# Identity products in half of the array's rows, the bias table in two passes of transfers, and two normalisations on GpSimd

## The chip, the cores and the metric

The kernel runs on one core of a Trainium2 chip. The metric is the device time of one launch in microseconds. Of the kernel before there are three runs, 289.52, 291.94 and 294.78 us (median 291.94), and one profiled execution of 286.88 us, whose span (first to last instruction) is 285.0 us.

## The reference

One transformer block in float32 on x of 8 batches x 256 tokens x 128 features:

```
n = layernorm(x)
q, k, v = split(n @ W_qkv + b_qkv)                  # 16 heads of 8
scores = q @ k.T / sqrt(8) + bias[head, i - j]      # rel_bias, clipped at +-128
y = softmax(scores) @ v @ W_out + b_out
x = x + layernorm(y)
h = silu(x' W1 s1) * (x' W2 s2)                     # x' = layernorm(x), ternary weights, 512 wide
h = gelu(h H1 s); h = gelu(h H2 s)                  # 512 x 512
x = x + layernorm(h W3 s)
```

## The kernel before, in words

**Stages.** A prologue (to about 34 us) normalises x, makes q and k in the layout that the scores need, and takes the row maxima of the scores of batch 0. Then seven loop passes b = 0 to 6 of eight slots s = 0 to 7 (a slot is a pair of heads) compute the attention of batch b and, beside it, the row maxima for batch b + 1. A last stage (about 173 to 190 us) does the attention of batch 7, and the feed-forward part (from about 190 us) works in four chunks of 512 tokens.

**One slot.** TensorE does, in this order: the scores of (b, s) on top of the bias (`scores`, L1325); the plain scores of (b + 1, s) (`max_scores`, L1291); the bias on top of these by a product of an identity with the table (`max_bias`, L1299); and then something that differs from slot to slot: the weighted sums of a group of four heads (`weighted`, L1351), transposes (`back`, `heads_T`, `norm_T`, `maxima_T`), the output projection (`project`, L1375), or in b = 0, 2, 3, 4 pieces of the q, k and v of later batches. L1325 and L1291 contract over 33 rows, at rows 0 and 64 of the array for the two heads of a pair; the identity product contracts over all 128 rows, two products of 512 columns in a slot.

VectorE takes the row maxima of the finished tile (`maxima`, L703). Then the tile is free for the bias of a later slot, copied from the table `raw` in SBUF by ScalarE (`write_bias`, L1053) or, in the slots of `BY_DVE`, by VectorE (L710). ScalarE takes the exponential of the scores (`probabilities`, L1046). There are three PSUM tiles `place`: ScalarE's copy of slot s waits for the maxima of slot s - 2, and the plain scores of slot s wait for the exponential of slot s - 1.

**Beside it.** In each pass b > 0 VectorE also finishes batch b - 1: `weigh` in s = 1, 2, `attn_moments` in s = 4 (adds the output bias, mean and variance), `residual` in s = 5 (normalises y, adds it to x, and takes mean and variance of the sum), `second_norm` in s = 6. GpSimd computes the inverse deviations between them (`inv_std`, L525), and in the pauses splits the feed-forward weights into a high and a low part (`split_weights`, eleven pieces, four instructions each, in the passes that `SPLIT_AT` gives).

**The table.** `ext` holds for each head one row of the bias by distance; `raw` is 128 partitions x 16 heads x 384, partition p shifted by p, loaded in eight transfers of 384 KB (L392) at the start. `table_hi` is its rounded copy in the format that the identity product reads, made by GpSimd (`table_high`, L533).

All engines run their lists in the order in which they are written, and so does SyncE, which issues nearly all transfers. Each PSUM tile, buffer and result has a semaphore.

## Time and profile before

| | us |
|---|---|
| runs | 289.52, 291.94, 294.78 |
| profiled execution | 286.88, span 285.0 |
| prologue | 0 to 34 |
| a loop pass (seven of them) | about 20.1 each, 34 to 173 |
| last attention stage, feed-forward part | 173 to 190, 190 to 285 |
| busy PE / DVE / ACT / POOL | 261.2 / 213.7 / 212.1 / 102.8 |

PE is TensorE, DVE VectorE, ACT ScalarE, POOL GpSimd, SP SyncE. A PE that counts as busy may still wait inside the array, since the ends of products are modelled. In a row of the timeline the first number is the start, the second the time from the first start to the last end of the group, and in brackets stands how long the engine had been idle, and for whom. A letter L with a number is a line of the kernel.

### The profile page before, as it was taken

The page shows a single profiled execution, that of the slowest core. Times are in us where ns is not written, and L with a number is a line of the kernel's source. Part 1 is how long each engine was busy: PE and PEld are TensorE (multiplying, and loading weights), DVE is VectorE, ACT ScalarE, POOL GpSimd, SP SyncE. Part 2 cuts the span into 40 slices and gives each one's busy share as a digit, 9 for nine tenths or more (in the row PEclk, how much of TensorE's full clock was granted, in tenths as well). Part 3 has the DMA queues.
Part 4 walks back from the last instruction along what each step waited for, and adds up shares of the span by engine and source line. Part 5 has one row for each costly group of instructions (what it writes and reads, how often), then busy time and mean ns, then how long its engine had stood idle before and what let it go on. Part 6 is the DMA issues. An engine that isn't in the chain of part 4 may idle for free.

```text
span 285.0 us, 5125 instructions
## 1 busy us (share of the span) xinstructions
PE 261.2 (92%) x1847; PEld 175.5 (62%) x1847; DVE 213.7 (75%) x443; ACT 212.1 (74%) x322; POOL 102.8 (36%) x107
## 2 busy tenths in 40 slices
PE   7899989999899998999998997788999999999980
PEld 7656645565555554555654654447888888888860
DVE  4676977989789889888898898859654853673576
ACT  2677777987878888887878878567469976896750
POOL 6716000101702603934986957017740302400111
PEclk9999999999999999999999999999999999999996
DMA  6979504522221355370322000000000000010012
GB/s 155 329 244 146 193 7 153 183 61 77 75 75 41 91 195 186 95 222 23 93 77 56 25 1 1 2 2 2 0 2 0 0 0 2 0 37 0 2 39 78
DMA packets 21356, 21.17 MB, mean 74 GB/s; under 512 B 3664, under 2 KB 18768, under 8 KB 21072
## 3 DMA queue, kind: packets, MB, share of 16 engines
q1 hardware_dynamic: 20464, 20.53, 24.8%
q10 hardware_dynamic: 864, 0.27, 0.5%
q8 instruction: 17, 0.28, 0.4%
q14 instruction: 11, 0.09, 0.1%
HBM read 14.90 MB, written 5.64 MB: 72 GB/s over the span
## 4 chain that ended last, share of the span: by engine, by line
PE 61%; DVE 20%; ACT 11%; issue 5%; POOL 1%; DMA 1%; ACTq 0%; POOLq 0%; DVEq 0%
PE place L1521 10%; PE place L1522 10%; PE place L1299 8%; DVE mx L703 7%; PE pv L1351 7%; ACT ring L1046 6%; PE place L1291 5%; PE place L1325 3%; DVE place L710 3%; ACT place L1053 2%; PE place L1250 2%; DVE stats L627 2%; PE misc L1229 2%; PE pv L1522 2%; PE misc L1362 2%
## 5 line engine op out<-in xcount | busy, mean ns | idle before, releaser
L703 DVE TENSOR_REDUCE mx<-place 128x4 f32<-128x1024 f32 x64 | 78.3, 1223 | 16.6 <-PE place L1299 15.2
L525 POOL TENSOR_TENSOR rstd<-mv,mhalf 128x2 f32<-128x2 f32 (+1 forms) x26 | 21.0, 806 | 143.2 <-DVE mv L635 143.1
L1046 ACT ACTIVATE ring<-place 128x1024 f32<-128x1024 f32 x64 | 65.5, 1028 | 1.1 <-PE place L1336 0.2
L1053 ACT COPY place<-raw 128x1024 f32<-128x1024 f32 x43 | 43.8, 1020 | 14.2 <-DVE mx L703 14.0
L1299 PE MATMUL place<-room,identr 128*128 128x512 f32 x128 | 46.9, 448 | 0.0
L1521 PE MATMUL place<-room,w_hi 128*128 128x512 f32 (+1 forms) x116 | 44.6, 387 | 0.7 <-DVE room L855 0.7
L1522 PE MATMUL place<-room,w_hi 128*128 128x512 f32 (+1 forms) x116 | 44.0, 382 | 0.0
L1325 PE MATMUL place<-room 33*128 33x256 f32 x256 | 31.9, 328 | 4.4 <-DVE place L710 2.9
L1351 PE MATMUL pv<-ring,vx 128*9 128x256 f32 x512 | 33.6, 380 | 0.7 <-ACT ring L1046 0.7
L855 DVE TENSOR_TENSOR room<-ring,room 128x512 fp32r<-128x512 f32 x32 | 21.3, 689 | 17.1 <-ACT room L1151 17.1
L1291 PE MATMUL place<-room 33*128 33x256 f32 x256 | 28.5, 299 | 4.1 <-ACT ring L1046 4.1
L1325 PEld LDWEIGHTS place<-room 33*128 33x128 f32 x256 | 19.2, 184 | 19.1 <-issue 13.7
L1291 PEld LDWEIGHTS place<-room 33*128 33x128 f32 x256 | 19.8, 185 | 11.6 <-issue 9.7
L710 DVE COPY place<-raw 128x1024 f32<-128x1024 f32 x20 | 24.2, 1225 | 1.0 <-ACT ring L1046 0.3
L1521 PEld LDWEIGHTS place<-room,w_hi 128*128 128x128 f32 x116 | 21.8, 188 | 5.1 <-DVE room L855 0.9
L1522 PEld LDWEIGHTS place<-room,w_hi 128*128 128x128 f32 x116 | 21.8, 188 | 4.1
L1299 PEld LDWEIGHTS place<-room,identr 128*128 128x128 f32 x128 | 19.0, 188 | 8.6
L1058 ACT COPY oT<-pv 128x256 f32<-128x256 f32 x32 | 11.8, 370 | 14.6 <-PE pv L1351 14.3
L1149 ACT ACTIVATE ring<-place,hs 128x512 f32<-128x512 f32 x27 | 18.5, 685 | 5.1 <-PE place L1522 5.1
L1351 PEld LDWEIGHTS pv<-ring,vx 128*9 128x9 f32 x512 | 11.0, 90 | 18.3 <-issue 11.3
L1151 ACT CAST room<-ring 128x512 fp32r<-128x512 f32 x32 | 19.9, 621 | 1.0
L1128 ACT ACTIVATE raw<-place,hs 128x512 f32<-128x512 f32 x16 | 11.0, 689 | 10.1 <-PE place L1522 9.7
(146 smaller groups left out, 422.7 us busy)
## 6 DMA issues: line engine op xcount, KB each, us to landing
raw<-ext SPq DMA_DIRECT2D x8, 384.0 KB, 6.6
room<-q_parts SPq DMA_DIRECT2D x48, 64.0 KB
room<-k_parts SPq DMA_DIRECT2D x48, 64.0 KB
w_lo<-h SPq DMA_DIRECT2D x2, 1024.0 KB, 5.6
q_parts<-w_hi SPq DMA_DIRECT2D x4, 256.0 KB, 3.0
k_parts<-w_hi SPq DMA_DIRECT2D x2, 512.0 KB, 3.7
xs<-x SPq DMA_DIRECT2D x3, 256.0 KB, 5.6
w_lo<-w SPq DMA_DIRECT2D x3, 256.0 KB, 2.9
```

Source lines behind the costliest of these rows:

```text
L525: nc.gpsimd.tensor_tensor(rstd[:, at:at + width], mv[:, at:at + width, 1], mhalf[:, 0:width], ALU.pow).then_inc(rstd_set, 1)
L703: nc.vector.tensor_reduce(mx[:, s // RPAIRS, :, :, s % RPAIRS].rearrange("p i k -> p k i"), max_tile(b * PAIRS + s)[:, :, :].rearrange("p ...
L710: nc.vector.tensor_copy(score_tile(i)[:, :, :].rearrange("p k (j n) -> p k j n", j=2), pair_windows(raw[:, :, :], i % PAIRS)).then_inc(bia ...
L855: nc.vector.tensor_tensor(lo, act_f[:, half[c], k, :], hi.bitcast(F32), ALU.subtract).then_inc((a1_lo_set, a2_lo_set)[i], 1)
L1046: nc.scalar.activation(probs[:, s % PRING, :, :, :].rearrange("p k j n -> p (k j n)"), score_tile(b * PAIRS + s)[:, :, :].rearrange("p k n ...
L1053: nc.scalar.copy(score_tile(i)[:, :, :].rearrange("p k (j n) -> p k j n", j=2), pair_windows(raw[:, :, :], i % PAIRS)).then_inc(bias_set, 1)
L1291: mm(max_tile(b * PAIRS + s)[:, half, it * S:(it + 1) * S], rows(q_rows, b, half, s)[:, it * P:(it + 1) * P], rows(k_rows, b, half, s), st ...
L1299: last = mm(max_tile(b * PAIRS + s)[:, half, :], identr[:, :], windows(table_hi[:, 2 * s + half, :], 0, P, 2, S), start=False, stop=True, ...
L1325: last = mm(tile[:, half, j * S:(j + 1) * S], rows(k_rows, b, half, s)[:, j * P:(j + 1) * P], rows(q_rows, b, half, s), start=(s in by_pe( ...
L1351: last = mm(pv[32 * r:32 * r + VC, 0:S], vx[:, b * TPB + j, 4 * g + r, :], probs[:, (2 * g + r // 2) % PRING, r % 2, j, :], start=(j == 0) ...
L1521: mm(o, w, hi, start=first, stop=False)
L1522: done = mm(o, w, lo, start=False, stop=last and exact)
```

## The change

1. The identity product is made in halves. The table for it holds for each pair one head in partitions 0 to 63 and the other in 64 to 127, 448 wide (384 + 64); a product contracts over 64 rows, and its identity (cut out of a 192-wide strip `ident_wide`, zeros around 64 diagonal columns) fills one half of the tile's 128 rows. So four products of 512 columns and 64 rows stand where two of 128 rows stood, the two heads in different halves of the array's rows.
2. This half table is loaded first, in eight transfers of 224 KB. The full `raw` is loaded later, four transfers after batch 1's parts have been stored and four after the row transfers of batch 1.
3. In the loop passes GpSimd does both normalisations and the addition to x (`residual`, `second_norm` on POOL); VectorE keeps the statistics (`x1_moments`, now in s = 6).
4. The splitting of weights is spread as two pieces a pass, W1 and W2 are loaded in the same pass, and H2's last pieces are split before H1's last.
5. In the last stage VectorE writes the bias of slots 2 and 3 before it weighs. TensorE gets four blank products in slot 7 of pass 1, and four where two were in pass 6.

```diff
-        table_hi = room[:, hi_at:lo_at].rearrange("p (h c) -> p h c", h=H)
+        raw_halves = w_lo[:, 2 * PAIRS * P:2 * PAIRS * P + PAIRS * TWIN].rearrange("p (s c) -> p s c", s=PAIRS)
+        table_hi = room[:, hi_at:lo_at].rearrange("p (s c) -> p s c", s=PAIRS)
...
-        SPLIT_AT = ((), (0,), (1,), (2, 3), (4, 5, 6), (7, 8, 9), (10,), ())
+        SPLIT_AT = ((), (0, 1), (2, 3), (8, 9), (4, 5), (6, 7), (10,), ())
...
+        def load_halves(eng, s):
+
+            eng.dma_start(raw_halves[:, s, :],
+                          bass.AP(tensor=ext.tensor, offset=2 * s * EXT,
+                                  ap=[[EXT, 2], [1, HP], [1, TWIN]])).then_inc(table_in[s], 16)
...
             store_parts(1)
+            for s in range(PAIRS // 2):
+                load_table(sp, s)
             sp.wait_ge(parts_out[1], PARTS_OUT)
             row_dmas(1, 0, PAIRS, second_rows_in)
+            send_mrow(sp, 0, 0)
+            for s in range(PAIRS // 2, PAIRS):
+                load_table(sp, s)
             load_x(4)
-            send_mrow(sp, 0, 0)
...
+            def residual(b):
+                inv_std(b * 2 + NU + 1, TPB)
+                pool.wait_ge(rstd_set, b * 2 + NU + 1)
+                for t in range(TPB):
+                    last = pool_normalize(y[:, t, :], y[:, t, :], t)
+                last.then_inc(y_norm, 1)
+                pool.wait_ge(y_norm, b + 1)
+                xb = xs[:, TPB * b:TPB * b + TPB, :]
+                nc.gpsimd.tensor_tensor(xb, xb, y[:, :, :], ALU.add).then_inc(x1_set, 1)
...
-                        if s == 5:
-                            residual(b - 1)
...
-                            second_norm(b - 1)
+                            x1_moments(b - 1)
...
             write_bias(first + 2)
+            write_bias(first + 3)
             weigh(B - 2, 0)
-            write_bias(first + 3)
...
+            def bias_product(tile, table, s, block, half):
+
+                at = half * HP
+                return mm(tile[:, half, :], ident_wide[at:at + HP, HP - block * HP:3 * HP - block * HP],
+                          windows(table[at:at + HP, s, :], block * HP, P, 2, S), start=False, stop=True,
+                          skip_group_check=True)
+
             def max_bias(b, s):
                 if b == 0:
                     pe.wait_ge(table_hi_pool, s + 1)
-                for half in range(2):
-                    last = mm(max_tile(b * PAIRS + s)[:, half, :], identr[:, :],
-                              windows(table_hi[:, 2 * s + half, :], 0, P, 2, S),
-                              start=False, stop=True, skip_group_check=True)
+                for block in range(2):
+                    for half in range(2):
+                        last = bias_product(max_tile(b * PAIRS + s), table_hi, s, block, half)
                 last.then_inc(ms_ready, 1)
...
-                        if b + 2 == B:
+                        if b in (1, B - 2):
                             pe.wait_ge(oT_set, (b + 1) * GROUPS - 1)
-                            stream(pv, blank, blank, 2)
+                            stream(pv, blank, blank, 4)
```

VectorE in slots 4 to 7 of pass 2, before (L703 the maxima, L638 and L745 the normalisations and the addition, L658 the low part of a later q):

```order
L731 TENSOR_TENSOR y_and_z<-misc,bo_bc 128x256
L627 BN_STATS stats<-y_and_z 128x6 x2
L631 BN_AGGR mv<-stats 128x2 x2
L635 TENSOR_SCALAR mv<-mv 128x2
L703 TENSOR_REDUCE mx<-place 128x2x2
L638 TENSOR_SCALAR y_and_z<-y_and_z,mv,rstd 128x128 x2
L745 TENSOR_TENSOR xs<-xs,y_and_z 128x256
L627 BN_STATS stats<-xs 128x6 x2
L631 BN_AGGR mv<-stats 128x2 x2
L635 TENSOR_SCALAR mv<-mv 128x2
L703 TENSOR_REDUCE mx<-place 128x2x2
```

and the same place now:

```order
L786 TENSOR_TENSOR y_and_z<-misc,bo_bc 128x256
L674 BN_STATS stats<-y_and_z 128x6 x2
L678 BN_AGGR mv<-stats 128x2 x2
L682 TENSOR_SCALAR mv<-mv 128x2
L757 TENSOR_REDUCE mx<-place 128x2x2 x2
L705 SCALAR_TENSOR_TENSOR w_hi<-misc,bq_sb,w_hi 128x512
L674 BN_STATS stats<-xs 128x6 x2
L678 BN_AGGR mv<-stats 128x2 x2
L682 TENSOR_SCALAR mv<-mv 128x2
L757 TENSOR_REDUCE mx<-place 128x2x2
```

The two maxima of slots 5 and 6 now follow each other, the statistics of x come behind the second, and four normalisations and an addition have left the engine.

TensorE in slots 4 to 6 of pass 1, now (L1390 the scores, L1350 the plain scores, L1357 the half products, L1416 the weighted sums, L1373 and L1283 transposes):

```order
L1440 MATMUL misc<-wo_sb,onT 128x128 x2
L1390 MATMUL place<-room 128x256 x4
L1350 MATMUL place<-room 128x256 x4
L1357 MATMUL place<-room 128x512 x4
L1373 MATMUL misc<-ident,mx 8x128 x2
L1390 MATMUL place<-room 128x256 x4
L1283 MATMUL misc<-ident,xn 128x128 x4
L1350 MATMUL place<-room 128x256 x4
L1357 MATMUL place<-room 128x512 x4
L1416 MATMUL pv<-ring,vx 9x256 x8
```

The order of the groups is as before; only the two identity products of a slot have become four, and what follows them is a product in all rows, as it was.

## Rows read from the trace of the kernel before

**Rows 1.** The page: busy times, and TensorE's granted clock in 40 slices.

```profile
PE 261.2 (92%) x1847; PEld 175.5 (62%) x1847; DVE 213.7 (75%) x443; ACT 212.1 (74%) x322; POOL 102.8 (36%) x107
PEclk9999999999999999999999999999999999999996
```

**Rows 2.** One pass: us, busy PE, PEld, DVE, ACT, POOL, then clock, DMA.

```profile
140.00:160.00 20.00, 18.64 (x172) 11.05 (x168) 17.10 (x32) 15.89 (x23) 15.79 (x15) 1.00 0.22 67
```

**Rows 3.** The chain of waits in pass 5: start us, us, what.

```profile
143.43 0.50 PE place L1291 x4
...
147.83 1.13 DVE mx L703
148.95 0.52 DVE y_and_z L638 x2
...
150.84 1.23 DVE mx L703
...
163.53 0.50 PE place L1291 x4
```

**Rows 4.** The chain of waits in pass 3.

```profile
101.70 0.68 PE place L1299 x2
...
102.40 1.24 DVE mx L703
...
108.32 1.13 PE misc L1229 x2
...
109.87 0.67 PE place L1299 x2
110.54 1.03 PE pv L1351 x16
```

**Rows 5.** Timeline of TensorE in pass 5, slots 6 and 7.

```profile
149.60 0.73 PE L1299 MATMUL place<-room,identr 128*128 128x512 f32 x2
...
151.59 0.40 PE L1291 MATMUL place<-room 33*128 33x256 f32 x4
151.92 0.73 PE L1299 MATMUL place<-room,identr 128*128 128x512 f32 x2
152.48 0.38 PE L1382 MATMUL misc<-ident,z_odd 128*128 128x128 f32 x2
```

**Rows 6.** One line's instructions, 80 to 160 us: durations min/median/max, first and last start.

```profile
L1299 PE MATMUL place<-room,identr x64: 389/448/503, 81.6 to 159.4; 128*128 128x512 f32 x64
L1291 PE MATMUL place<-room x128: 272/277/384, 81.2 to 158.8; 33*128 33x256 f32 x128
```

**Rows 7.** Groups of GpSimd by line, 80 to 160 us: count, busy us, mean ns, idle before.

```profile
L585 POOL TENSOR_SCALAR w_hi<-w_lo 128x512 fp32r<-128x512 f32 x8 | 12.0, 1504 | 0.7
L577 POOL TENSOR_TENSOR w_lo<-w_lo,w_hi 128x512 f32<-128x512 f32 x8 | 10.3, 1285 | 0.6
L525 POOL TENSOR_TENSOR rstd<-mv,mhalf 128x2 f32<-128x2 f32 x8 | 5.7, 714 | 33.9 <-DVE mv L635 33.8
L575 POOL CAST w_hi<-w_lo 128x512 fp32r<-128x512 f32 x8 | 4.9, 614 | 5.9 <-DVE z_odd L638 3.3 <-DVE y_and_z L638 2.6
```

**Rows 8.** Timeline of the prologue: TensorE and ScalarE in one of its slots, SyncE later.

```profile
15.76 0.84 ACT L1005 ACTIVATE room<-place,brows_sb 128x256 fp32r<-128x256 f32 x2 [0.59 <-PE place L1257]
...
16.63 1.02 ACT L997 ACTIVATE z_parts<-place,low_bias,brows_sb 128x256 fp32r<-128x256 f32 x2
...
25.91 1.23 SPq L400 DMA_DIRECT2D room<-mrow  x2
```

**Rows 9.** Timeline of the last stage and of the feed-forward part's start.

```profile
179.34 0.50 PE L1325 MATMUL place<-room 33*128 33x256 f32 x4 [1.81 <-DVE place L710]
...
181.33 0.76 PE L1325 MATMUL place<-room 33*128 33x256 f32 x8
...
188.90 0.73 POOL L525 TENSOR_TENSOR rstd<-mv,mhalf 128x2 f32<-128x2 f32 x1 [11.05 <-DVE mv L635]
...
193.51 0.38 PE L1382 MATMUL misc<-ident,y_and_z 128*128 128x128 f32 x2
```

More of the change, by code:

```diff
@@ L23 @@
 EXT = WIN + P - 1
+HP = P // 2
+TWIN = WIN + HP
 CH = 512
@@ L243, in build @@
         rows_set = sem("rows_set")
+        table_in = [sem(f"table_in{s}") for s in range(PAIRS)]
         table_hi_pool = sem("table_hi_pool")
@@ L337, in build @@
         WPIECES = WCOLS // WPIECE
-        SPLIT_AT = ((), (0,), (1,), (2, 3), (4, 5, 6), (7, 8, 9), (10,), ())
+        SPLIT_AT = ((), (0, 1), (2, 3), (8, 9), (4, 5), (6, 7), (10,), ())
+        SPLIT_ORDER = [piece for pieces in SPLIT_AT for piece in pieces]
         def wait_gate_low(eng, c, k):
@@ L585, in split_weights, with pool_normalize, second_norm @@
                 nc.gpsimd.tensor_scalar(is_0, w_lo[:, cols], 0.0, None, ALU.is_equal).then_inc(w_low_is_0_set, 1)
[L586 removed]
+                pool.wait_ge(w_low_is_0_set, n + 1)
                 nc.gpsimd.tensor_tensor(w_low_all_0, w_low_all_0, is_0 if last else is_0.bitcast(F32),
                                         ALU.mult).then_inc(w_low_all_0_set, 1)
+            def pool_normalize(dst, src, t):
+                return nc.gpsimd.tensor_scalar(dst, src, mv[:, t, 0:1], rstd[:, t:t + 1], ALU.subtract, ALU.mult)
+            def residual(b):
[7 more added lines that the diff above has]
+                nc.gpsimd.tensor_tensor(xb, xb, y[:, :, :], ALU.add).then_inc(x1_set, 1)
+            def second_norm(b):
+                inv_std(b * 2 + NU + 2, TPB)
+                pool.wait_ge(rstd_set, b * 2 + NU + 2)
+                if b > 1:
+                    pool.wait_ge(zT_ready, b - 1)
+                for t in range(TPB):
+                    last = pool_normalize(z[b][:, t, :], xs[:, b * TPB + t, :], t)
+                last.then_inc(z_set, 1)
+            split = 0
             for b in range(B):
                 if b > 0:
[L592 to L597 removed]
+                    residual(b - 1)
+                    second_norm(b - 1)
+                for _ in SPLIT_AT[b]:
+                    split_weights(split)
+                    split += 1
             def gate_parts(c):
@@ L1333, in score_bias @@
                 pe.wait_ge(table_lo_set, low + 1)
-                for half in range(2):
-                    for part in (table_hi[:, 2 * s + half, :], table_lo[:, 2 * low + half, :]):
-                        last = mm(score_tile(b * PAIRS + s)[:, half, :], identr[:, :], windows(part, 0, P, 2, S),
-                                  start=False, stop=True, skip_group_check=True)
+                for table, at in ((table_hi, s), (table_lo, low)):
+                    for block in range(2):
+                        for half in range(2):
+                            last = bias_product(score_tile(b * PAIRS + s), table, at, block, half)
                 last.then_inc(st_ready, 1)
```

85 lines of the change are left out of this document (47 added, 38 removed).

## The prediction

> **What bounds the kernel now.** I began with the page [rows 1]. TensorE is busy 92% of the span and its clock is granted in full in every slice but the last, so there is no clock to win, only some to lose. But VectorE and ScalarE stand at 75 and 74% over the whole, and more where the change is made: in a pass of the loop TensorE is busy 18.64 of 20 us, VectorE 17.10, ScalarE 15.89 [rows 2]. Three engines so close together hold each other in turn, so I read the chain of waits for single passes. Two kinds of pass show. In pass 5 the chain enters VectorE with the statistics of y and stays there through two maxima, with the normalisation, the addition and the statistics of x between them: the first maxima end at 148.95, the second start at 150.84 [rows 3]. One period is 163.53 - 143.43 = 20.10 us. Passes 1 and 6 look like this too. In pass 3 (and 2 and 4) TensorE has a piece of q, k or v in slot 6 (1.13 us at 108.32), and the chain runs over that piece and the identity product behind it, past VectorE's block [rows 4]. There, taking work off VectorE shortens nothing by itself.
>
> **The half products.** Follow one slot of TensorE in [rows 5]: plain scores from 151.59, identity products from 151.92, the next work in all rows from 152.48; together 0.89 us. The plain scores are four products of 256 columns and last 0.40 us, while one lasts 0.28 [rows 6], so the last starts only 0.12 after the first: two abreast in the two halves of the rows, a pair every 0.12 us, and the weights of the second pair are loaded under the first. The streaming of the scores is over at 151.59 + 0.24 = 151.83, and the identity product starts 0.1 later. Its two products need 0.73 us in all, and the shorter lasts 0.39 [rows 6], so they start 0.34 apart, 0.1 more than the 0.24 that twice 256 columns take: the first one's weights are loaded in the open. Going from halves to all rows costs 0.2 us. Now the change: four half products are two pairs of 512 columns, 2 x 0.24 = 0.48 us, directly behind the scores. Their result is ready 0.2 us earlier. For TensorE itself the crossing isn't gone, it only comes after the identity product, because in every slot of the loop something in all rows follows: 0.24 + 0.48 + 0.1 to 0.2 = 0.82 to 0.92 us against 0.89. I take 0.1 us less where a load of 9 columns or an identity follows; the bounds are 0.2 less and nothing.
>
> On the path this counts by where the product leads. In pass 3 it leads to VectorE's maxima twice (101.70 and 109.87, 0.2 us each) and to TensorE's own next work three times (0.1 each): **0.7 us**. Three such passes: -2.1. Pass 0 has no batch to finish and long products in slots 2 to 6; I take -0.5 for it.
>
> **The normalisations on GpSimd.** VectorE loses four normalisations and an addition: two take 0.52 us [rows 3], the other two as much, and with an addition of about 0.4 that is some 1.5 us a pass. In pass 5 what counts is the gap of 1.89 us between the maxima of slots 5 and 6 [rows 3]. It can shrink only to when the tile of slot 6 is ready: before at 149.60 + 0.73 = 150.33 [rows 5], now 0.2 earlier through the half products and 0.2 more because the slots before are earlier, 149.9. So 0.9 us of 1.89 come back. With 0.3 us for products elsewhere on that chain, **1.2 us** a pass. Pass 6 has 0.1 more, since the second normalisation also stood on its chain. Pass 1 gives 0.4 back for its four new blank products, which cover an idle piece only in part. Sum for passes 1, 5 and 6: -0.8 - 1.2 - 1.3 = -3.3.
>
> GpSimd's price has to be bounded. No row shows it normalising 128 x 128 with two scalars per partition. A cast of 512 columns takes 0.61 us and a compare 1.50 [rows 7]; a quarter of them would be 0.15 and 0.38, the whole compare 1.50. I take 0.5, near the quarter of the compare, which is the same kind of instruction, plus a start-up; the ends are 0.15 and 1.5. The addition is half of a 1.29 us one, 0.7. After the mean and variance (147.8) that is 0.7 for the power + 1.0 + 0.7 + three hand-overs = 2.7 us: x is ready at 150.5. VectorE asks for it at the end of the slot 6 maxima, 149.9 + 1.2 = 151.1. So it is hidden with 0.6 us to spare. If that cover goes, the price is taken by slot 7's maxima. The splitting of weights waits behind the second normalisation on GpSimd: two pieces are 2 x (0.61 + 1.29 + 1.50 + 1.29) = 9.4 us, plus gaps; GpSimd's whole pass is then about 9.8 + 4.9 = 15 us of 19, and no longer three pieces (14 us) in one pass. It costs nothing. VectorE's new wait before the statistics of y is for a normalisation that ended most of a pass ago.
>
> **The table, the prologue.** Casts on GpSimd shrink, but they never were on the path. In a prologue slot ScalarE spends 0.84 + 1.02 us and waits 0.59 for the product L1257 in between [rows 8], a ring of 2.45 us that the identity product is not in; TensorE gains nothing there. VectorE writes a wider identity, three small copies more, before anything waits for it: 0. The transfers: 1.75 MB of half tables instead of 3 MB first, then 1.5 MB before batch 1's rows, then the first row of maxima, which was issued at 25.91 [rows 8] while the loop starts at 34, and four tables behind that. There are 8 us of slack for 0.25 MB more. I cost this at 0; if it failed, all passes would shift by what the rows of batch 1 come after 34 us.
>
> **The last stage.** TensorE waits 1.81 us for VectorE's bias of slot 3 at 179.34 [rows 9]. The new order writes it before the weighing, so slot 3 starts 1.7 us earlier, but slot 5's bias still needs the same VectorE work before it, and slots 4 and 5 ran together at 181.33. I take -0.4, between 0 and -1.7.
>
> **The start of the feed-forward part.** Here the residual of batch 6 stands in the open: from GpSimd's power at 188.90 to the transposes at 193.51 [rows 9]. GpSimd's normalisations and addition are longer than VectorE's by 2 x 0.4 + 0.3 = 1.1 us. TensorE has some idle time to absorb it; I take +0.7, with 0 and +4 (at 1.5 us each) as ends.
>
> **Sum.** -2.1 - 0.5 - 3.3 - 0.4 + 0.7 = **-5.6 us**: 286.88 to 281.3 for the profiled execution. The median of the runs is 5.1 us above that execution, and I put the change against it: 291.94 - 5.6 = **286.3 us**. About 2% (5.8 us) is what a measurement of this kernel tells from no change, so my own figure lies at that edge.
>
> **The rivals.**
>
> *A larger gain.* Once TensorE's products come sooner and VectorE is 1.5 us emptier, the ring of the tiles turns faster in all six passes: the product of a slot, its maxima, the bias, the exponential, and the plain scores that wait for that. For it: the wait of TensorE is part of the 1.4 us of idle time that a pass has [rows 2]. Against it: in passes 2 to 4 the block was off the chain. Six passes at 1.3 with pass 0 as above and the rest unchanged: -7.8 - 0.5 + 0.4 - 0.4 + 0.7 = -7.6, with the slots earlier in the next pass perhaps -9. About 283. Chance 0.27.
>
> *Off the path.* ScalarE is the next to bind, with 15.9 us busy and a fixed order; the 0.9 us of passes 1, 5 and 6 are lost to it, and the 0.1 us for TensorE too. Left are 0.2 us twice in each of seven passes, -2.8, and +0.7: -2, 290. Chance 0.17.
>
> *GpSimd becomes the bound* (the slower side). Place: slot 6 of passes 1 to 6. VectorE ended slot 6's maxima at 150.84 + 1.23 = 152.07 and then normalised for 0.5, so slot 7 began at 152.6. The statistics take the 1.89 us of the gap less 0.52 and 0.4, or 0.95; they must begin by 151.7, 3.9 us after GpSimd is called. That is the point: 1.1 us for a normalisation. At the upper end of 1.5 us x comes at 147.8 + 0.7 + 3.0 + 1.3 = 152.8, and slot 7 is 1.1 us later than before: +6.6 in six passes, less 2 for the products, and +3.5 at the start of the feed-forward part: +8, 300. Against it: the compare of four times the size takes 1.50. Chance 0.07.
>
> *The change doesn't do what it says:* the halves do not run abreast. Four products of 512 columns one after another add 0.48 us to each slot, against TensorE's 1.4 us of idle time in a pass: some +2.5 in each of seven passes, 308. The scores do run abreast with the same halves. Chance 0.04.
>
> *Weights in the open.* If the weights of the second pair had to wait for the first, which uses the same rows, each pair would cost 0.1 us more, the results would be no earlier, and TensorE would lose 0.1 us a slot: only 0.5 us in each of passes 1, 5 and 6 is left, about -1, 291. The plain scores speak against it, 0.12 us apart [rows 5, 6]. Chance 0.05. The Trainium skill, "TensorE: Matmul & The Clock Gate", Part 3, says that a weight load overlaps a product in flight only when its row group differs; by that rule it would come out so, and the trace disagrees.
>
> **How the numbers follow.** The forecast itself has 0.40, half of it beyond 2%. Faster: 0.19 + 0.27 = 0.46. Within 2%: 0.21 + 0.17 + 0.05 = 0.43. Slower: 0.11. The range leaves out the two slower rivals and the far end of the large gain: 279 to 293; it takes in the bounds of the products, of the last stage, and a normalisation of up to about 1.0 us.
>
> **What would show it.** Half products that start in pairs, with 0.5 us of streaming for four and the maxima 0.2 us sooner; passes of 19.4 us (2 to 4) and 18.9 us (1, 5, 6); the maxima of slots 5 and 6 with 1 us or less between them; GpSimd's normalisation near 0.5 us; the clock still granted in full. I am wrong if a normalisation takes over 1 us, if the passes 2 to 4 shorten as much as the others, or if the clock falls in a pass where TensorE has more idle time than now.

## The result, and the profile after

The changed kernel takes **317.97 us** (median of 4 runs, 315.50 to 320.12) against 290.73 us of the kernel before on the same chip (4 runs, 288.88 to 294.78): ratio 1.0957 [1.0822, 1.1093], slower by 9.6%. I had forecast 286.3 us, in a range of 279 to 293. The profiled execution took 319.23 us, with a span of 317.4 us. Where a ratio stands below, it leaves out runs over 1.5% above the fastest of their kernel; of the kernel before these are most on some chips, so the medians, which keep them, are given beside it.

Stage by stage, from the starts of the first scores and of the transposes of `heads_T` (slot 3 of each pass; period 1 runs from slot 3 of pass 1 to slot 3 of pass 2, and so on). h3 is the changed kernel with only its table transfers mended; it comes below.

| us | before | after | h3: table mended |
|---|---|---|---|
| first scores of the loop | 33.20 | 60.97 | 32.93 |
| from there to slot 3 of pass 1 | 28.96 | 30.84 | 27.67 |
| then period 1 | 19.98 | 18.91 | 18.91 |
| periods 2, 3, 4 | 20.06, 20.07, 20.12 | 19.38, 19.38, 19.35 | 19.38, 19.38, 19.36 |
| period 5 | 20.11 | 18.88 | 18.87 |
| period 6, into the last stage | 20.81 | 22.27 | 19.96 |
| from there to batch 6's `norm_T` | 10.20 | 13.68 | 12.48 |
| to the end | 91.49 | 93.74 | 92.16 |

Periods 1 to 5 shorten about as forecast. 27.8 us are lost before the loop and 1.9 in pass 0. Another 7.2 us are lost behind period 5: there the granted clock is 0.50 from 204 to 212 us. In h3, whose clock is full there, the same three rows lose 2.1.

The page of the changed kernel, answering to [rows 1], shows TensorE idle from about 48.5 to 61 us (slices of 7.9 us), and its clock near 0.5 in most slices from 24 to 71; below are two lines of its DMA part (KB each, median us from issue to landing; none is given for the half tables):

```profile
PE 272.9 (86%) x1985; PEld 180.5 (57%) x1985; DVE 202.3 (64%) x411; ACT 211.0 (66%) x322; POOL 126.6 (40%) x142
...
PEclk9985585559999999999999999759799999999996
...
raw<-ext SPq DMA_DIRECT2D x8, 384.0 KB, 10.7
...
w_lo<-ext SPq DMA_DIRECT2D x8, 224.0 KB
```

Windows of ten us of the changed kernel (columns as in [rows 2]; the last three are granted clock, share of the 16 DMA engines, GB/s):

```profile
10.00:20.00 10.00, 8.70 (x50) 5.94 (x50) 6.06 (x19) 8.08 (x19) 2.08 (x3) 1.00 0.14 52
20.00:30.00 10.00, 7.64 (x26) 4.82 (x26) 1.59 (x3) 3.36 (x8) 1.12 (x3) 0.61 0.22 74
30.00:40.00 10.00, 8.45 (x29) 4.58 (x30) 5.33 (x16) 3.94 (x10) 2.08 (x3) 0.54 0.30 108
50.00:60.00 10.00, 0.00 (x0) 0.00 (x0) 0.00 (x0) 1.02 (x1) 0.00 (x0) 0.50 1.13 194
```

The same window of the kernel before:

```profile
10.00:20.00 10.00, 9.51 (x48) 6.26 (x48) 5.92 (x18) 8.17 (x19) 5.05 (x6) 1.00 0.85 286
```

From 10 to 20 us the DMA engines are at 14% and move 52 GB/s, where they were at 85% and 286. 0.14 of 16 is 2.2 engines. The transfers have not run out: the waits of GpSimd and TensorE up to 62 us (us in total, times, longest) and the timelines of GpSimd, SyncE and TensorE show who waits for them:

```profile
POOL room L558 <- DMA w_lo<-ext: 30.7, 8, 4.8
```

```profile
PE place L1390 <- DMA room<-mrow: 12.4, 1, 12.4
PE place L1357 <- POOL room L558: 5.9, 4, 2.8
```

```profile
10.50 0.56 POOL L558 CAST room<-w_lo 128x448 fp32r<-128x448 f32 x1 [2.05 <-DMA w_lo<-ext]
15.89 0.56 POOL L558 CAST room<-w_lo 128x448 fp32r<-128x448 f32 x1 [4.84 <-DMA w_lo<-ext]
...
45.01 0.56 POOL L558 CAST room<-w_lo 128x448 fp32r<-128x448 f32 x1 [4.42 <-DMA w_lo<-ext]
```

```profile
22.05 9.89 SPq L403 DMA_DIRECT2D w_lo<-ext  x3
31.98 4.44 SPq L460 DMA_DIRECT2D q_parts<-z_parts  x1
...
50.17 1.32 SPq L416 DMA_DIRECT2D room<-mrow  x2
```

```profile
60.97 0.80 PE L1390 MATMUL place<-room 33*128 33x256 f32 x4 [12.45 <-DMA room<-mrow]
```

Eight half tables are cast between 10.50 and 45.01 us: one every 34.5 / 7 = 4.9 us, 224 KB each, one after another. GpSimd's cast waits for each, TensorE's identity product for the cast. Worse, SyncE issues in order and is held itself: the issue of three half tables takes 9.89 us. The row of maxima was issued at 25.91 [rows 8]. ScalarE now has it ready at 34.5:

```profile
34.12 0.36 ACT L1089 CAST mrow<-misc 8x256 fp32r<-8x256 f32 x1 [2.69 <-PE misc L1373]
```

But it is issued at 50.17, behind the store of batch 1's parts, four full tables and the row transfers of batch 1. By the trace's landing events it lands at 60.92, right behind the last of those rows (60.54). TensorE waits 12.45 us for it and the loop starts at 60.97, at 1.2 GHz.

**Why 4.9 us.** The source of a half table is written `[[EXT, 2], [1, 64], [1, 448]]`: the two heads first, then 64 rows. The trace gives three completion events for such a transfer, the last two of them at its end (44.61 and 44.95 us for the eighth), and sixteen for those of the kernel before, and two engines' worth of load. The Trainium skill, "DMA: Bandwidth & Descriptors", section "Why a DMA increments its semaphore by 16 and not by 1", states the rule: a transfer is spread over the largest number of engines up to 16 that divides the slowest dimension of both sides. These are 128 in the tile and 2 in the source, so it is 2. The trace agrees, with its 0.14 and its three events.

**The passes.** The changed kernel, answering to [rows 2], [rows 5] and [rows 3]: a window of one pass, the timeline of TensorE in slot 7, and of VectorE from slot 5 to slot 7 of pass 5.

```profile
168.00:188.00 20.00, 18.87 (x198) 10.96 (x194) 16.11 (x29) 17.00 (x24) 16.10 (x17) 1.00 0.18 56
```

```profile
177.75 0.41 PE L1350 MATMUL place<-room 33*128 33x256 f32 x4
178.00 0.63 PE L1357 MATMUL place<-room 64*128 64x512 f32 x4
178.56 0.44 PE L1447 MATMUL misc<-ident,z_odd 128*128 128x128 f32 x2
```

```profile
176.54 1.23 DVE L757 TENSOR_REDUCE mx<-place 128x4 f32<-128x1024 f32 x1 [1.34 <-PE place L1357]
177.68 0.48 DVE L674 BATCH_NORM_STATS2 stats<-xs 128x6 f32<-128x128 f32 x2
...
178.67 1.23 DVE L757 TENSOR_REDUCE mx<-place 128x4 f32<-128x1024 f32 x1
```

The four half products last 0.63 us, start 0.25 after the plain scores (before 0.33), and end 178.63 - 177.75 = 0.88 after these start, where it was 152.65 - 151.59 = 1.06. Between the maxima lie 178.67 - 177.77 = 0.90 us, before 1.89 [rows 3]. VectorE is at 16.11 us of 20.

**GpSimd and the last stage** (groups of GpSimd in the loop and behind it, as [rows 7]; then the timeline of TensorE and of GpSimd that answers to [rows 9]):

```profile
L616 POOL TENSOR_SCALAR y_and_z<-y_and_z,mv,rstd 128x128 f32<-128x128 f32 x14 | 11.1, 797 | 0.8
L626 POOL TENSOR_TENSOR xs<-xs,y_and_z 128x256 f32<-128x256 f32 x7 | 5.1, 732 | 0.6
```

```profile
207.42 0.80 PE L1390 MATMUL place<-room 33*128 33x256 f32 x4 [1.09 <-DVE place L765]
...
223.66 0.66 PE L1447 MATMUL misc<-ident,y_and_z 128*128 128x128 f32 x2 [2.09 <-POOL y_and_z L616]
```

```profile
216.80 0.72 POOL L550 TENSOR_TENSOR rstd<-mv,mhalf 128x2 f32<-128x2 f32 x1 [11.76 <-DVE mv L682]
217.62 1.58 POOL L616 TENSOR_SCALAR y_and_z<-y_and_z,mv,rstd 128x128 f32<-128x128 f32 x2
219.28 0.74 POOL L626 TENSOR_TENSOR xs<-xs,y_and_z 128x256 f32<-128x256 f32 x1
```

A normalisation takes 0.797 us (I took 0.5), the addition 0.73 (0.7). From the power to the transposes it is 223.66 - 216.80 = 6.86 us, before 193.51 - 188.90 = 4.61. TensorE's wait for a bias, 1.81 us at slot 3 before [rows 9], now stands at slot 5 (1.09 us at 207.42).

### The profile page after: what moved, and what is told of

It is laid out like the page before. It is cut to its first block, busy times and chain, and to the rows that moved or that the text cites. A ratio compares the mean times of both kernels' runs of the same rounds, so it can differ in the third digit from the quotient of the medians.

```text
span 317.4 us, 5479 instructions
## 1 busy us (share of the span) xinstructions
PE 272.9 (86%) x1985; PEld 180.5 (57%) x1985; DVE 202.3 (64%) x411; ACT 211.0 (66%) x322; POOL 126.6 (40%) x142
## 3 DMA queue, kind: packets, MB, share of 16 engines
q1 hardware_dynamic: 21504, 22.37, 23.9%
## 4 chain that ended last, share of the span: by engine, by line
PE 50%; DVE 14%; SPq 13%; ACT 8%; issue 6%; DMA 6%; POOL 2%; ACTq 0%; DVEq 0%; POOLq 0%
PE place L1586 9%; PE place L1587 9%; PE pv L1416 7%; DVE mx L757 6%; SPq L403 5%; PE place L1357 5%; ACT ring L1104 4%; PE place L1390 4%; PE place L1350 3%; DMA room<-mrow 3%; DVE place L765 3%; DMA k_parts<-z_parts 3%; PE misc L1427 2%; SPq L424 2%; ACT place L1112 2%
## 5 line engine op out<-in xcount | busy, mean ns | idle before, releaser
L1104 ACT ACTIVATE ring<-place 128x1024 f32<-128x1024 f32 x64 | 65.6, 1027 | 13.3 <-PE place L1390 11.8
L1357 PE MATMUL place<-room 64*128 64x512 f32 x264 | 45.8, 426 | 5.9 <-POOL room L558 5.9
L1390 PE MATMUL place<-room 33*128 33x256 f32 x256 | 34.0, 345 | 14.5 <-DMA room<-mrow 12.7
L1586 PE MATMUL place<-room,w_hi 128*128 128x512 f32 (+1 forms) x116 | 44.7, 387 | 0.7 <-DVE room L912 0.7
L1390 PEld LDWEIGHTS place<-room 33*128 33x128 f32 x256 | 20.4, 196 | 30.2 <-DMA room<-mrow 13.2
L1416 PE MATMUL pv<-ring,vx 128*9 128x256 f32 x512 | 35.9, 401 | 0.4 <-ACT ring L1104 0.4
L1350 PE MATMUL place<-room 33*128 33x256 f32 x256 | 30.5, 316 | 4.3 <-ACT ring L1104 4.3
L1350 PEld LDWEIGHTS place<-room 33*128 33x128 f32 x256 | 21.1, 198 | 12.8 <-issue 11.4
L1357 PEld LDWEIGHTS place<-room 64*128 64x128 f32 x264 | 22.8, 204 | 7.0 <-POOL room L558 6.8
L1416 PEld LDWEIGHTS pv<-ring,vx 128*9 128x9 f32 x512 | 11.2, 92 | 19.5 <-issue 13.1
L1117 ACT COPY oT<-pv 128x256 f32<-128x256 f32 x32 | 11.8, 370 | 13.1 <-PE pv L1416 13.0
```

The source lines that it names most:

```text
L1104: nc.scalar.activation(probs[:, s % PRING, :, :, :].rearrange("p k j n -> p (k j n)"), score_tile(b * PAIRS + s)[:, :, :].rearrange("p k n ...
L1350: mm(max_tile(b * PAIRS + s)[:, half, it * S:(it + 1) * S], rows(q_rows, b, half, s)[:, it * P:(it + 1) * P], rows(k_rows, b, half, s), st ...
L1357: return mm(tile[:, half, :], ident_wide[at:at + HP, HP - block * HP:3 * HP - block * HP], windows(table[at:at + HP, s, :], block * HP, P, ...
L1390: last = mm(tile[:, half, j * S:(j + 1) * S], rows(k_rows, b, half, s)[:, j * P:(j + 1) * P], rows(q_rows, b, half, s), start=(s in by_pe( ...
L1416: last = mm(pv[32 * r:32 * r + VC, 0:S], vx[:, b * TPB + j, 4 * g + r, :], probs[:, (2 * g + r // 2) % PRING, r % 2, j, :], start=(j == 0) ...
L1586: mm(o, w, hi, start=first, stop=False)
```

## The experiments: the table

**f1_halves16** and **f2_swapped** mend the order of the source in two ways. f2 swaps two dimensions, which puts the same numbers of bytes in other partitions (its table is therefore not the reference's); f1 loads each half by a transfer of its own, and two or three pairs in one.

```diff
# f2_swapped
-                                  ap=[[EXT, 2], [1, HP], [1, TWIN]])).then_inc(table_in[s], 16)
+                                  ap=[[1, HP], [EXT, 2], [1, TWIN]])).then_inc(table_in[s], 16)
# f1_halves16, for half in range(2); pairs 0, 1-2, 3-4, 5-7 together
+                                  ap=[[1, HP], [2 * EXT, n], [1, TWIN]])).then_inc(table_in[s], 16)
```

> The changed kernel, with the half tables loaded by one transfer per half (64 partitions, source [64 rows, pairs, 448]) instead of one per pair (source [2 heads, 64 rows, 448]); the same bytes, eight transfers. Theory A: the 28 us before the loop come from the shape of the source, whose slowest dimension of 2 puts a transfer on two of the sixteen DMA engines (224 KB then take some 5 us). Then the loop starts at 33 to 35 us instead of 61, and the time is 284 to 290 us. Rival B: they come from the order and the amount (half tables first, raw tables before the rows of batch 1). Then the loop still starts after 50 us and the time stays over 305. Rival C: they come from the lower granted clock between 20 and 40 us: the loop starts at about 50.

> The changed kernel with one thing else: the source of each half table transfer is read in the order [64 rows, 2 heads, 448] instead of [2 heads, 64 rows, 448]. Count, bytes and runs of 1792 B are the same, but the table's rows land in other partitions, so the bias in the maxima and in one slot of the last batch is not the right one. Theory A: it runs on sixteen engines and the loop starts at 33 to 35 us, time 284 to 290. Rival B and a rival by which runs of 1792 B are slow in themselves: as the changed kernel, 315 to 320.

f1: 284.41 us (282.75 to 287.57, 4 runs; ratio 0.961 [0.9542, 0.9678] to the kernel before, 295.11 on this chip). f2: 285.16 us (2 runs), ratio 0.9654 [0.956, 0.9748]. In f2 one line is other than in the changed kernel, and the loop starts at 32.98. Its DMA line, its window and its first scores against the ones above:

```profile
w_lo<-ext SPq DMA_DIRECT2D x8, 224.0 KB, 4.0
```

```profile
10.00:20.00 10.00, 9.12 (x54) 6.21 (x54) 6.53 (x20) 8.05 (x19) 3.03 (x5) 1.00 0.93 274
```

```profile
32.98 0.50 PE L1390 MATMUL place<-room 33*128 33x256 f32 x4
```

Sixteen events a transfer, all eight landed by 14.9 us instead of 45. **f3_three_slow** keeps the changed kernel's form for the first three half tables only:

> The first three half tables by the two-engine shape, the other five by the sixteen-engine one. Theory A, 4.6 to 4.9 us for each of eight transfers one after another: the third lands at 18 to 20 us, the rest within 5 us behind it, and the loop starts at 36 to 42 us; time 288 to 297. Rival B: over 305.

298.42 us (2 runs), ratio 1.0103 [1.0015, 1.0191]. The loop starts at 44.72:

```profile
44.72 0.80 PE L1395 MATMUL place<-room 33*128 33x256 f32 x4 [4.57 <-DMA room<-mrow]
```

Both lie outside what I had expected (36 to 42 us, and 288 to 297). The third half table is cast at 23.71, not by 20, and the row of maxima is waited for once more. Still, the loop starts at 33.0, 44.7 and 61.0 with none, three and eight slow transfers, so each costs 3.5 to 3.9 us of the start. **h1_before_two_engines** does only the harm, in the kernel before (its table values, as in f2, lie in other places of the tile than the reference wants):

```diff
-                                  ap=[[1, P], [EXT, 2], [1, WIN]])).then_inc(raw_in[s], 16)
+                                  ap=[[EXT, 2], [1, P], [1, WIN]])).then_inc(raw_in[s], 16)
```

> The kernel before with one line changed: the source of its 384 KB table transfers counts the two heads first and the 128 rows second (its values so land in other places of the tile; sizes and counts are the same). Theory (a transfer spreads over as many DMA engines as divide its slowest dimension, here two): each takes 384/224 of the 4.9 us that a half table took in the changed kernel, 8.4 us, eight of them one after another end near 72 us, and the loop starts near 85 us instead of 33: 340 us, slower by some 50. Rival (the loss of the changed kernel lies in its half tables or in its new order of transfers, not in the order of the source's dimensions): no change, 293 us.

349.65 us (2 runs; 340 was expected), profiled span 345.1. The first scores of the loop start at 84.15 us; 85 was expected. That is 51 of the 60 us by which the span is longer; the other 9 are lost behind it, most of them where the windows show a fallen clock (0.51 from 84 to 94 us, 0.59 from 210 to 214). The first scores, and the last casts of GpSimd:

```profile
84.15 0.80 PE L1325 MATMUL place<-room 33*128 33x256 f32 x4 [8.27 <-DMA room<-mrow]
```

```profile
64.13 0.82 POOL L533 CAST room<-raw 128x768 fp32r<-128x768 f32 x1 [6.95 <-DMA raw<-ext]
72.06 0.83 POOL L533 CAST room<-raw 128x768 fp32r<-128x768 f32 x1 [7.11 <-DMA raw<-ext]
```

The last two are 7.9 us apart; from the first cast (13.29) to the eighth it is 58.8 us, 8.4 for each 384 KB. 4.9 for 224 would give 8.4. So the cause is shown from both sides: taken out of the change, the order of the source's dimensions gives the loss back; put into the kernel before, it makes one.

## The experiments: the normalisations

**f4_norms_dve** is f1 with all normalisations and additions back on VectorE; the half products, the spread pieces and the blank products stay.

> As the first kernel (sixteen-engine shape), but the two normalisations and the addition are back on VectorE in all batches. Theory: GpSimd's part gives 0.5 us in each of passes 1, 5 and 6 and costs about 2 us at the start of the feed-forward part, where its normalisation of 0.79 us instead of 0.30 stands in the open: this kernel is within 1 us of the first. Rival: GpSimd's part is worth 1.2 us in every pass: this kernel is 5 us or more slower than the first.

284.07 us (282.21 to 284.90, 4 runs), ratio 0.9614 [0.9538, 0.9691]: no different from f1. But stage by stage it is: its periods are 19.40 us in all five, where f1 has 18.92 and 18.87 in periods 1 and 5 and 19.38 between. So the half products give 0.6 to 0.7 us in every pass (together with the spread pieces; the two were not taken apart), GpSimd's part another 0.5 in two, and what is lost again stands in the open ahead of the feed-forward part, which the next run shows. **g2_last_on_dve** (with **h3** and **h4**, f1 and g2 again side by side) takes batch 6 alone back to VectorE:

```diff
-                if b > 0:
+                if 0 < b < B - 1:
                     residual(b - 1)
                     second_norm(b - 1)
+                if b == B - 1:
+                    inv_std((b - 1) * 2 + NU + 1, TPB)
+                    inv_std((b - 1) * 2 + NU + 2, TPB)
...
             any_low()
+            residual(B - 2)
+            x1_moments(B - 2)
             z_low(B - 3)
-            x1_moments(B - 2)
+            second_norm(B - 2)
```

> The changed kernel with its table over sixteen DMA engines, and with the two normalisations and the addition of batch 6 (those of the last stage) back on VectorE; batches 0 to 5 stay on GpSimd. Theory: GpSimd's 0.80 us for a normalisation pays in passes 1, 5 and 6, where it takes work off the chain, and costs at the start of the feed-forward part, where TensorE waits 2.1 us for it. So passes as in the kernel with all of them on GpSimd (18.9 in 5 and 6), the transposes of batch 6 about 1.5 us earlier after the last stage began: 282.5 us against 284.4. Rival: the start of the feed-forward part is set by VectorE's other work there; then no change, 284 us.

> The changed kernel with its table over sixteen DMA engines once more, beside the version with batch 6's normalisations on VectorE, on one chip. Theory: 1.5 to 2 us slower than that version, 284 us. Rival: the same, since what one saves at the start of the feed-forward part the other had absorbed.

> The version with batch 6's normalisations on VectorE once more, beside the one with all of them on GpSimd. Theory: 282.1 us again, 1.5 to 2 us below it, and the fastest of all kernels here, 0.97 of the kernel before. Rival: 284, the same as it.

g2: 282.12 us (281.07 to 282.49, 4 runs), ratio 0.9743 [0.9625, 0.9861] (before there: median 292.95). Side by side, h4 took 281.85 us (280.52 to 283.74, 6 runs), ratio 0.9695 [0.959, 0.9799], and h3 284.58 (282.39 to 287.74, 6 runs), ratio 0.9781 [0.9661, 0.9901], against a median of 296.4. The 2 us are there (2.7 in these medians, 2.3 in the profiles' stage ahead of the feed-forward part: 12.48 us in h3, 10.21 in g2, both at full clock), though single runs of the two overlap. h4 (with j1, below, its equal) is the fastest version: its longest run (283.74) is below the shortest of the kernel before (289.02). TensorE in h3, at the place where h4 has no such wait:

```profile
188.94 0.41 PE L1445 MATMUL misc<-ident,y_and_z 128*128 128x128 f32 x2 [2.10 <-POOL y_and_z L614]
```

**h2_pool_only** puts the normalisations on GpSimd in the kernel before and changes nothing else; **i3_pool_spread** spreads the weights' splitting as well.

```diff
# i3 on top of h2
-        SPLIT_AT = ((), (0,), (1,), (2, 3), (4, 5, 6), (7, 8, 9), (10,), ())
+        SPLIT_AT = ((), (0,), (1,), (2, 3), (4, 5), (6, 7), (8, 9, 10), ())
```

> The kernel before with only the normalisations and the addition of batches 0 to 5 moved to GpSimd; table, products and the order of VectorE's biases as before. Theory: passes 1, 5 and 6, where the block stood on the chain, gain 0.5 to 0.9 us each, passes 2 to 4 nothing (20.1), so about 2 us: 290.5 us against 292.9. Rival: without the half products the tile of slot 6 is ready only at 150.33, so no more than 0.5 us of the gap comes back and that is lost to ScalarE: no change.

> The kernel with only the normalisations of batches 0 to 5 on GpSimd, and the splitting of the weights spread (two pieces in passes 3 to 5 and three in the sixth, in place of three in passes 4 and 5). Theory: in the version before this one VectorE waited 2.2 us in pass 5 for an addition that stood behind a third piece on GpSimd, and the clock fell after it; without that wait passes 5 and 6 are 20.1 us or less, and the kernel is 8 to 10 us faster than that version and no slower than the kernel before: 289 to 293 us. Rival: the normalisation at 0.80 us itself is too long without the half products, and pass 5 still waits: 297 us.

h2: 299.68 us (296.46 to 303.89, 4 runs), ratio 1.0313 [1.0092, 1.0533], and 3.3 us above the median of 296.4, with runs that overlap. A gain of 2 us or no change was expected, and neither came. It is my GpSimd rival, by another door. VectorE and GpSimd in pass 5 of h2:

```profile
152.12 1.23 DVE L727 TENSOR_REDUCE mx<-place 128x4 f32<-128x1024 f32 x1 [1.57 <-PE place L1327]
155.51 0.49 DVE L651 BATCH_NORM_STATS2 stats<-xs 128x6 f32<-128x128 f32 x2 [2.16 <-POOL xs L601]
```

```profile
150.99 1.29 POOL L587 TENSOR_TENSOR xn<-xn,w_hi 128x512 f32<-128x512 f32 x1
152.24 0.72 POOL L525 TENSOR_TENSOR rstd<-mv,mhalf 128x2 f32<-128x2 f32 x1
```

GpSimd's power starts at 152.24, when its third piece is done, although the variance was there at 149.4. The addition comes 2.2 us late for VectorE, and TensorE's clock falls behind it. With the pieces spread (i3), period 5 is 19.69 instead of 24.22 us, and GpSimd waits for VectorE again. So the normalisations on GpSimd need the spreading of the pieces, in the kernel before at least; with half products it was not tried without. I had called it free and did not ask what would happen without it. As a whole i3 took 295.55 us (10 runs), ratio 1.0133 [1.0074, 1.0191], median of before 295.10: no gain. Its profiled execution, the longest of the ten (300.19), has the clock fallen in period 1 (24.24 us) and in the last stage. I had expected 289 to 293 us, 8 to 10 below h2; it is 4 below, and only the wait in pass 5 went as I said.

## The experiments: the clock

The mended kernels gain 9 to 15 us in the medians; my sum had 5.6. **g1**, **i1** and **i2** are the kernel before, unchanged, for more profiles of it.

> The kernel before, unchanged, for a second profile of it. The kernels with the table over sixteen DMA engines stand 11 us below it in the comparisons, but their profiles only 4 to 5 us below the profile of before that the prediction used. Theory one: that profile was a good execution, and a usual one loses some 8 us more, in one piece, where TensorE's clock falls to 1.2 GHz (a slice with a granted clock near 0.5) or in the transfers ahead of the loop. Theory two: the loss is spread, and every pass is a few tenths over 20.1 us. If neither shows and the span is again 285 us, the difference lies in what surrounds the span.

> The kernel before unchanged, for a profile of one of its longer executions (most of its runs took 293 to 297 us at a mean clock of 0.95 to 0.97, some 289 at 0.985). Theory: the 8 us between them are stretches of a few us in which TensorE's clock stands at 1.2 GHz, at one or two places of the loop where TensorE idles for VectorE, and every pass without one is again 20.1 us. Rival: the loss is in passes that are longer at full clock.

> The same once more, in case the first profile falls on a short execution. If both show fallen clock in the same pass, the place belongs to the program; if in different passes, to chance.

They took 289.43, 295.08 and 295.70 us. The page's clock of i1, against the last line of [rows 1]:

```profile
PEclk9999999999799999999997999579999999999995
```

i1 against the profile of the prediction, by the stages of the table above: periods 21.50 (+1.52), 20.06, 20.07, 20.12, 21.58 (+1.47), 22.42 (+1.61), then 12.77 (+2.57) and 92.35 (+0.86). That is 8.0 of the 8.2 us. i2 loses in period 5 (21.63), in period 6 (22.26) and behind it (15.21 where it was 10.20), not in 1. Each lies where the clock is at 1.2 GHz for a few us. Three windows of each, first the kernel before as the prediction saw it, then i1:

```profile
72.00:74.00 2.00, 1.00 (x8) 0.51 (x8) 1.43 (x2) 2.00 (x3) 1.65 (x3) 1.00 0.08 23
74.00:76.00 2.00, 2.00 (x23) 0.85 (x23) 0.95 (x1) 1.61 (x2) 1.91 (x2) 1.00 0.47 140
76.00:78.00 2.00, 2.00 (x16) 1.34 (x16) 1.84 (x3) 1.67 (x3) 1.59 (x2) 1.00 0.36 105
```

```profile
72.00:74.00 2.00, 1.01 (x6) 0.42 (x6) 1.59 (x3) 2.00 (x3) 1.49 (x3) 1.00 0.03 8
74.00:76.00 2.00, 1.99 (x14) 0.95 (x18) 0.32 (x1) 1.78 (x2) 1.91 (x2) 0.62 0.50 143
76.00:78.00 2.00, 2.00 (x20) 0.46 (x12) 1.97 (x2) 0.37 (x1) 1.72 (x2) 0.52 0.40 116
```

Nearly the same work at the same time, TensorE idle for 1.0 us of two at the seam of passes 1 and 2, where it waits for ScalarE twice; in one execution the clock stays, in the other it falls. At the seams behind passes 2 to 4 TensorE is busy for 1.55 to 1.64 us of two, and no profile of the kernel before shows a fall there. Two tests of whether blank products matter (their results are used by nothing, they only keep TensorE busy):

```diff
# j2_before_blanks, in the kernel before; j1_no_blanks takes both blank pieces out of g2
-                        if b + 2 == B:
+                        if b in (1, B - 3, B - 2):
                             pe.wait_ge(oT_set, (b + 1) * GROUPS - 1)
-                            stream(pv, blank, blank, 2)
+                            stream(pv, blank, blank, 4)
```

> The version with the table over sixteen DMA engines and batch 6's normalisations on VectorE, without any blank products in slot 7 of passes 1 and 6 (there were four in each). Theory: TensorE's clock falls in the kernel before because it is idle for 1.0 us of two at the start of the pass after 1, and for 0.6 to 0.8 after pass 5; half products and GpSimd's share shorten that idle time by themselves, so the clock stays full in passes 1 and 5, where there is no blank product in the second; only pass 6 and the last stage may fall: 282 to 284 us. Rival: the blanks hold the clock; then pass 1 falls in most runs and costs 1.5 us, the last stage 1.6 more: 285 to 288 us.

> The kernel before with four blank products at the end of slot 7 in passes 1, 5 and 6 (it had two, in pass 6). Theory: they fill the idle piece after which the clock fell in the profiles of its longer runs, and passes 1 and 5 are 20.1 us in every run, 3 us saved of the 8 by which those runs exceed the shortest; the last stage and the start of the feed-forward part stay as they are: 291 to 292 us, with mean clocks of 0.97 and up in place of 0.95 to 0.96. Rival: the blanks (0.45 us each four) are on TensorE's path or do not keep the clock: 295 us or more, no change.

j2: 291.60 us (288.61 to 293.50, 6 runs) against 295.12 (289.00 to 297.82, 11 runs) of the kernel before, its first five periods in the profile 20.00 to 20.12: the 291 to 292 expected. The shortest runs of the two are alike (288.61 and 289.00): what differs is how many runs are long. TensorE at the seam of j2 is busy for 1.47 us of two:

```profile
72.00:74.00 2.00, 1.47 (x12) 1.03 (x11) 1.55 (x3) 2.00 (x3) 1.53 (x3) 1.00 0.04 11
```

j1: 281.81 us (281.50 to 283.78, 6 runs), as good as with them (h4 281.85, on another chip). But my reason for it falls: at its seam TensorE is nearly as idle as before the change, and the clock stays.

```profile
70.00:72.00 2.00, 1.08 (x11) 0.70 (x11) 1.44 (x3) 1.98 (x3) 1.57 (x3) 1.00 0.04 14
```

So blank products do help the kernel before, as far as 6 runs against 11 tell, the changed one does without, and less idle time isn't the whole of it. Why its passes hold the clock stays open.

**g3_old_last_order** and **g4_blanks** vary the last stage of g2 (the old order of VectorE's biases; eight blank products ahead of slot 5):

```diff
# g3
             write_bias(first + 2)
-            write_bias(first + 3)
             weigh(B - 2, 0)
+            write_bias(first + 3)
             write_bias(first + 4)
+            write_bias(first + 5)
             weigh(B - 2, 1)
-            write_bias(first + 5)
# g4
+            pe.wait_ge(oT_set, (B - 1) * GROUPS + 1)
+            stream(pv, blank, blank, 8)
             last_scores(5)
```

> The kernel of g2 with the order of VectorE's work in the last stage as the kernel before had it (bias of slot 3 behind the first weighing, the second weighing behind the bias of slot 5). My prediction gave the new order 0.4 us. If that holds, this kernel is 0.4 us slower. Rival: the new order opens a stretch in the last stage in which TensorE idles and its clock falls to 1.2 GHz (it did in every profile of the changed order, at 172 to 184 us); then the old order is faster by 1 to 2 us, and its granted clock there stays near 1.00.

> The kernel of g2 with eight blank products of TensorE ahead of slot 5 of the last stage, which fill an idle piece of it. If the fallen clock in the last stage costs time, the blanks keep it at 2.4 GHz and the last stage and the start of the feed-forward part are 1 to 2 us shorter. Rival: the clock falls for the idle time before that, or the stage is set by VectorE and ScalarE, whose work does not depend on TensorE's clock; then no change, or up to 0.5 us slower for the blanks themselves.

g3 283.51 us (282.81 to 284.57), g4 282.91 (280.68 to 285.44), g2 282.12 (281.07 to 282.49), 4 runs each. The medians give the new order 1.4 us, and the blanks nothing that can be told. In the profile of g3 the clock fell in the last stage (172 to 176 us, 0.63), in that of g2 not; it did in that of its twin h4 (0.59). The order doesn't decide it, and most of the 1.4 us is clock. At the same mean clock (0.984 and 0.985) g3 has 282.81 and 282.99 us, g2 282.28 and 282.49: 0.5 us. The rows say the same. From the scores of slot 2 of the last stage to the transposes of `heads_T`, both at full clock, first the kernel before, then g2:

```profile
176.44 0.50 PE L1325 MATMUL place<-room 33*128 33x256 f32 x4 [0.47 <-DVE place L710]
183.31 0.44 PE L1369 MATMUL misc<-ident,on 128*128 128x128 f32 x2
```

```profile
170.22 0.50 PE L1393 MATMUL place<-room 33*128 33x256 f32 x4 [0.62 <-DVE place L766]
176.63 0.44 PE L1437 MATMUL misc<-ident,on 128*128 128x128 f32 x2
```

These are 6.87 and 6.41 us, so the stage gained 0.46.

## Why the prediction was wrong

- **The step that failed** is "There are 8 us of slack for 0.25 MB more. I cost this at 0." I compared bytes and the order of issues, and took for granted that 224 KB travel as fast per byte as 384 KB did. The diff shows both descriptions; the new one has the 2 in front. It cost 27.8 us ahead of the loop and 1.9 in pass 0; f2, with this one line put the other way round, starts the loop at 32.98. The sentence behind it, on what a failure would do (all passes shift by what the rows of batch 1 come after 34 us), was right, since these rows land at 60.54, 26.5 us after 34, and it got neither a price nor a chance. No rival held it, so nothing in the range could. The 8 us of slack were true: f1 and f2, with the new order of transfers, start the loop no later than before.
- **Passes 2 to 4**, forecast -0.7 each: -0.68, -0.69, -0.77. **Passes 1 and 5**, forecast -0.8 and -1.2: -1.07 and -1.23. The sizes came out, the shares did not, so there is some luck in them. The result of a slot comes 0.18 us earlier (0.2 forecast), TensorE's own next work 0.81 after the plain scores (0.82 to 0.92). f4 splits them: products 0.6 to 0.7 everywhere; GpSimd 0.5 more where VectorE's block led the chain. In pass 5 I had put 0.9 of the 1.2 to the gap between two maxima; the products give 0.7 by themselves (f4). In pass 1 I had given 0.4 back for the blank products; j1, without them, has the same period (18.91).
- **Pass 0**, forecast -0.5: -1.3 in h3 (with slots 0 to 2 of pass 1). Under-sized; f4, with the normalisations on VectorE, has it too (27.68 us).
- **GpSimd's normalisation**, 0.5 taken, 0.80 measured: hidden in the passes, not at the start of the feed-forward part, where I forecast +0.7 within 0 to +4 and h3 shows 12.48 - 10.20 = +2.3. Behind it h3 takes 0.7 us more (92.16 against 91.49), for which I had no term and have no cause. I had put it near a quarter of the compare's 1.50; it is half of it.
- **The last stage**, forecast -0.4: -0.46 from slot 2 on (g2), about as forecast. Slot 3 no longer waits, and slot 5 does, as I had said.
- **Pass 6**, forecast -1.3: over-sized. Period 6, which holds most of it and the last stage, went from 20.81 to 19.96 in h3, -0.85 for both together, where -1.7 was forecast. Why is open.
- **"There is no clock to win, only some to lose."** Wrong, and on the sheet: the median of the runs stood 5.1 us above the profiled execution, and I added this difference to my result as if it were fixed. i1 shows it is fallen clock in periods 1, 5 and 6 and in the last stage. The mended change wins most of it back. In executions at nearly full clock (mean 0.991 and up) the kernel before took 286.88 and 287.68 us and h3 282.98 and 282.39, so about 4 to 5 us are the program's, and the rest of the 11.8 in the medians is clock.
- **Rivals.** A larger gain: no, passes 2 to 4 gave 0.7 and not 1.3. Off the path: no, passes 1 and 5 gave 1.1 and 1.2. Halves abreast: yes, no rival there. Weights in the open: no, half products of the same rows follow each other without the 0.1 us. GpSimd as the bound: not in this kernel, but 4 us in h2, through its queue and not through the price of an instruction. With the table mended, the changed kernel is h3: -3.9 us in the spans (285.0 to 281.1), -11.8 in the medians on that chip; the forecast of -5.6 lies between. That h3's median (284.58) falls inside my range is in part luck: the clock helped, and I had put it at nothing.

## What to carry to other kernels

Read a moved transfer's access pattern, not its size: put the rows of the tile outermost on both sides (64 or 128 of them gave sixteen completion events here), and a pair index of 2 behind them (outermost it gave three). The sign in a profile is a low DMA share while the issuing queue is blocked: 0.14 and 52 GB/s here. When the median stands some us above the profiled execution, take another profile before adding the difference to a forecast. And when a queue in order gets a short job on the path, ask which long job may stand ahead of it.

## What the runs showed of the hardware that I had not expected

- A 224 KB transfer with a slowest dimension of 2 takes 4.9 us, a 384 KB one 8.4 (7.9 to 8.8, h1). The same 224 KB as 64 rows x 2 heads land 4.0 us after their issue (median in f2), as 64 rows x 2 pairs 4.6 (f1), several at once. While such transfers are open, others on the same queue are held: the issue of a 256 KB load of x lasted from 16.35 to 22.00, fourteen of its sixteen completion events came at 23.9 to 24.7 us, and the last two at 30.2 and 30.7, behind the half table issued before it (29.9). That these two shares stood behind it on the same two engines is inferred.
- TensorE's clock can fall at one and the same place in one execution and not in another (the windows at 74 us above). Of 11 runs of the kernel before in the last comparison one had a mean granted clock of 0.985 (289.00 us), ten 0.951 to 0.965 (292.54 to 297.82).
- GpSimd: `tensor_scalar` with two scalars per partition on 128 x 128 takes 0.80 us, a compare on 128 x 512 1.50 [rows 7]: a quarter of the elements for half of the time.
